# Cross attention 0: value products of two key tiles together; maxima kept in a table; keys copied ahead of the accumulator; other slots in the cosformer

## The chip, the cores and the metric

The kernel runs on one core of a Trainium2 chip. Its time is the device time of one execution in microseconds (us). A core has five engines with an instruction stream each, all in order: TensorE (PE in the profile, its weight loads PEld), VectorE (DVE), ScalarE (ACT), GpSimd (POOL) and SyncE (SP, which starts DMAs). They wait for one another by semaphores alone. SBUF holds operands; matmuls write to PSUM, which has eight banks of 128 partitions x 512 float32.

## The reference

A four-layer decoder on x of 1024 tokens x 128; each layer has a self attention, a cross attention over 6404 context rows, and a feed-forward part. The change touches two of the twelve parts. The first is the cross attention of layer 0 ("cross 0"), with 16 heads of 64:

```python
qw = (q_in @ Wq + bq).reshape(B, M, HEADS, QSIZE)
kw = (k_in @ Wk + bk).reshape(B, N, HEADS, QSIZE)
vw = (v_in @ Wv + bv).reshape(B, N, HEADS, KSIZE)
a = jnp.einsum('bmhd,bnhd->bhmn', qw, kw) / jnp.sqrt(jnp.float32(QSIZE))
a = jnp.where(key_mask[:, None, None, :], a, -jnp.inf)
a = jax.nn.softmax(a, axis=-1)
o = jnp.einsum('bhmn,bnhd->bmhd', a, vw).reshape(B, M, HEADS * KSIZE)
return o @ Wo + bo
```

The second is the self attention of layer 1, a "cosformer": queries and keys go through a relu and are weighted by the cosine and sine of their position, and a causal linear attention follows (16 heads of 64):

```python
num = jnp.einsum('bhi,bhij->bhj', qc, S_cos) + jnp.einsum('bhi,bhij->bhj', qs, S_sin)
den = jnp.sum(qc * z_cos + qs * z_sin, axis=-1)
den = jnp.maximum(den, 1e-06)[..., None]
return ((S_cos, S_sin, z_cos, z_sin), num / den)
```

## The kernel before, in words

**Cross 0** works on P = 8 pairs of heads, one after another; the two heads of a pair sit in partitions 0 to 63 and 64 to 127. The 6404 keys are C = 13 chunks of 512 (the last has 260), which are KT = 51 key tiles of 128: four to a chunk, three in the last. So there are N = 104 chunks in all and 408 tiles, counted by t over all pairs. Since 51 is odd, the tile that begins a chunk has an even t in pairs 0, 2, 4, 6 (called even pairs below) and an odd t in pairs 1, 3, 5, 7 (odd pairs).

Softmax needs each query's maximum before the exponentials. So two passes run at once, one chunk of each in a "turn" (`turns`, line 2188 on): the maxima pass works on chunk g, and the scores pass on chunk j = g - 14 (LAG is 14). Turns with g from 0 to 13 have maxima alone, g from 14 to 103 have both (90 turns), g from 104 to 117 have scores alone. A turn has as many steps s as chunk j has tiles. On PE (from line 2302) a step is, in order:

- `maxima(g, q)` (L2223): scores of query tile q of 128 against the chunk's 512 keys, in bf16, for both heads, to a pair of PSUM banks. There are eight q to a turn, so two to a step of four. While scores run too, they all use banks 4 and 5 (`maxima_bank`). DVE reduces both banks to one maximum for each head (L2405), and only then may PE write there again: `take_banks(4, ...)` waits for whoever used these banks last.
- `scores(j, s, half)` for both halves of the queries (L2236 in float32, L2238 which subtracts the maxima by a product with ones), to banks 0 and 1, and 2 and 3. ACT takes the exponential of each half into `Pr` (L2342), which has four slots by t.
- In step 0, one maxima call stands between the halves, and then `keys_and_values` (L2262, L2267) makes the next chunk's keys into bank 4 and values into bank 5; ACT copies the keys twice (L2362 float32, L2365 bf16) and the values once (L2371).
- Once for each pair, in a step of its own: `queries` (the projection), `rows` (maxima turned into rows), `sums` (row sums), `output`. All of these use banks 4 and 5 too.
- `products(t - 1)` (L2255): the values times the exponentials of the tile before, added up in banks 6 and 7.

The step's second maxima call stands behind the scores, right ahead of the products. POOL adds every exponential tile to the row sums (L2462, L2471). DVE merges the turn's maxima into `mx` (L2434 for the first chunk of a pair, L2437 later); at a pair's end it also negates them, rounds them to bf16 and keeps the rest (L2441, L2445, L2447), for `rows`. At a pair's end ACT copies the accumulator (L2356), once the pair's last products are done, ahead of the key copies of that step.

**The cosformer** (line 670 on) again has P = 8 pairs of heads, each with 12 units (PER): a unit u is up to 512 queries against a key tile of 128. PE makes the scores of unit n (L796), then one of the side jobs, then the products of unit n - 2 (L810). The side jobs all use banks 4 and 5 and stand at fixed u: queries and keys of the next pair (L767, L778), values in pair 0 (L785), column sums (L819), spreading of the inverted sums (L826) and the output projection (L833). DVE weights the scores (L948) and serves the side jobs between: values (L910), bound and inverse of the sums (L916 on, L921), scaling (L926), adding to X (L933, L935).

## Time and profile before

| | |
|---|---|
| three runs | 6390.63, 6393.21, 6397.06 us |
| profiled execution | 6391.79 us, its span 6390.0 us |
| mean granted TensorE clock | 0.915 |
| PE busy in the span | 5378.6 us, 84% |
| DVE, ACT, POOL busy | 3074.3, 3079.3, 2202.5 us |

The page of the profile gives this. A timeline shows the instructions of one engine in order of time, equal ones merged: start, duration, engine, line, what it writes and reads, the count, and in brackets how long the engine sat idle before it and who ended that wait. The duration of a merged matmul row runs to its modelled end, so it overlaps the next row's start; distances between starts are what counts. Cross 0's scores run from about 510 us to 2745 us of the span, the cosformer's loop from 2911 us to 3175 us.

### The profile page before, as it was taken

Reading aid. Unit: us, or ns where it says so; the run is one execution under the profiler, and the core shown is the slowest. Engines: PE = TensorE matmul, PEld = TensorE weight load, DVE = VectorE, ACT = ScalarE, POOL = GpSimd, SP = SyncE. Lnnn points to the kernel's source line nnn. Section 1 sums busy time; section 2 is a strip of 40 time slices with the busy share of each in tenths; the row PEclk is TensorE's granted clock in tenths of the full one; section 3 lists DMA queues with packets and bytes.
Section 4 is the critical chain, followed back from the end, with each engine's and each line's share of the span. In section 5 each row is a group of like instructions: output and inputs, shape, how many; then the busy total and the mean of one; then the engine's idle time right before and its main releaser. Section 6 shows DMA issues by size and latency. Waiting matters only on the chain. (4 is left out here: it accounts for less than half of the span.)

```text
span 6390.0 us, 69096 instructions
## 1 busy us (share of the span) xinstructions
PE 5378.6 (84%) x27758; PEld 1715.5 (27%) x27772; DVE 3074.3 (48%) x3482; ACT 3079.3 (48%) x3081; POOL 2202.5 (34%) x1100
## 2 busy tenths in 40 slices
PE   6658999999898999988888579998983588888879
PEld 2213333333333333332243211111431111111124
DVE  6575554555555554014541500000156999998613
ACT  3214444444454445521022379998121177777842
POOL 1006887878787878934533000000000000000000
PEclk7859999999999999989999789999796599999979
DMA  1000000000000000000000210000003000000001
GB/s 41 14 0 1 1 1 1 1 1 1 1 1 1 1 1 1 1 18 20 2 0 5 73 50 14 13 10 8 17 23 115 19 10 10 10 10 11 1 19 33
DMA packets 64814, 89.16 MB, mean 14 GB/s; under 512 B 9791, under 2 KB 49780, under 8 KB 62894
## 3 DMA queue, kind: packets, MB, share of 16 engines
q1 hardware_dynamic: 64494, 84.73, 4.2%
q8 instruction: 220, 3.60, 0.2%
q14 instruction: 100, 0.82, 0.0%
HBM read 59.33 MB, written 25.38 MB: 13 GB/s over the span
## 5 line engine op out<-in xcount | busy, mean ns | idle before, releaser
L2405 DVE TENSOR_REDUCE red<-ps 128x2 f32<-128x1024 f32 (+1 forms) x832 | 976.6, 1181 | 968.4 <-PE ps L2223 966.4
L2342 ACT ACTIVATE Pr<-ps,key_bias 128x1024 f32<-128x1024 f32 x816 | 897.6, 1115 | 1113.9 <-PE ps L2238 1111.4
L2462 POOL TENSOR_TENSOR Ps<-Ps,Pr 128x1024 f32<-128x1024 f32 x400 | 945.7, 2364 | 321.5 <-ACT Pr L2342 321.5
L2898 DVE TENSOR_REDUCE red<-ps 128x2 f32<-128x1024 f32 (+2 forms) x1102 | 961.3, 926 | 81.3 <-PE ps L2813 67.9
L2471 POOL TENSOR_TENSOR Ps<-Ps,Pr 128x1024 f32<-128x1024 f32 x400 | 949.9, 2375 | 32.8 <-ACT Pr L2342 32.7
L2876 ACT ACTIVATE Pr<-ps 128x1024 f32<-128x1024 f32 x816 | 786.2, 1021 | 226.4 <-PE ps L2823 225.3
L2236 PE MATMUL ps<-Q,Kr 64*128 64x512 f32 x3264 | 852.8, 601 | 0.0
L492 POOL MEMSET sel<- 16x2048 f32 (+1 forms) x2 | 2.7, 1368 | 2434.2 <-POOLq L89 2434.2
L2255 PE MATMUL ps<-Pr,Vc 128*64 128x512 f32 x3264 | 789.8, 605 | 0.0
L3001 ACT ACTIVATE Pr<-ps 128x2048 f32<-128x2048 f32 x467 | 726.2, 2025 | 1.6 <-PE ps L2967 1.6
L2813 PE MATMUL ps<-Kp,Q 52*128 52x512 bf16 (+1 forms) x1664 | 450.5, 411 | 225.0 <-DVE red L2898 149.1
L2223 PE MATMUL ps<-Kb,Qb 64*128 64x512 bf16 (+1 forms) x1664 | 332.6, 402 | 151.3 <-DVE red L2405 117.1
L2836 PE MATMUL ps<-Pr,V 128*9 128x512 f32 x3264 | 436.4, 606 | 0.0
L2980 PE MATMUL ps<-Pr,V 128*8 128x512 f32 x3264 | 427.2, 595 | 0.5 <-ACT Pr L3001 0.5
L2823 PE MATMUL ps<-Q,Kp 52*128 52x512 bf16 x1632 | 363.8, 386 | 12.2 <-ACT Pr L2876 11.8
L2236 PEld LDWEIGHTS ps<-Q,Kr 64*128 64x128 f32 x3264 | 312.2, 191 | 161.6 <-issue 122.7
L3010 DVE COPY Oc<-ps 128x512 f32<-128x512 f32 x8 | 5.5, 692 | 725.0 <-PE ps L2980 725.0
L2967 PE MATMUL ps<-Q,Kp 48*128 48x512 bf16 x1632 | 283.6, 385 | 82.6 <-ACT Pr L3001 55.2
L2813 PEld LDWEIGHTS ps<-Kp,Q 52*128 52x128 bf16 x1664 | 107.2, 94 | 799.9 <-DVE red L2898 712.8
L2238 PE MATMUL ps<-Qa,ones 64*128 64x512 bf16 x1632 | 313.7, 380 | 0.0
L2255 PEld LDWEIGHTS ps<-Pr,Vc 128*64 128x64 f32 x3264 | 198.0, 136 | 382.0 <-issue 290.5
L2223 PEld LDWEIGHTS ps<-Kb,Qb 64*128 64x128 bf16 x1664 | 80.4, 95 | 664.9 <-DVE red L2405 420.8
(563 smaller groups left out, 5245.8 us busy)
## 6 DMA issues: line engine op xcount, KB each, us to landing
L_dram_K<-parts SPq DMA_DIRECT2D x26, 384.0 KB, 2.9
Kp<-L_dram_K SPq DMA_DIRECT2D x16, 624.0 KB
L_dram_K<-parts SPq DMA_DIRECT2D x26, 256.0 KB, 2.4
Kp<-L_dram_K SPq DMA_DIRECT2D x16, 416.0 KB
w<-L_ffn_experts_w_dram SPq DMA_DIRECT2D x24, 256.0 KB, 3.0
ctx<-ctx_dram SPq DMA_DIRECT2D x13, 256.0 KB, 5.3
L_dram_K<-parts SPq DMA_DIRECT2D x26, 128.0 KB, 1.7
keep<-L_dram_mask SPq DMA_DIRECT2D x13, 256.0 KB, 3.5
```

The costliest lines, as they stand in the source:

```text
L2236: nc.tensor.matmul(ps[:, 2 * half + a, :], lhsT=Kr[head(a), j % 16, s * 128:(s + 1) * 128], rhs=Q[head(a), p % 3, sl], start=True, stop=False)
L2255: mm = nc.tensor.matmul(ps[head(a), 6 + half, :], lhsT=Vc[:, j % 3, at:at + 64], rhs=Pr[:, t % 4, half, a, :], start=False, stop=True, ski ...
L2342: nc.scalar.activation(Pr[:, t % 4, half].rearrange("p a n -> p (a n)"), ps[:, 2 * half:2 * half + 2, :].rearrange("p a n -> p (a n)"), AC ...
L2405: nc.vector.tensor_reduce(red[:, g % 2, q, :], ps[:, maxima_bank(g, q):maxima_bank(g, q) + 2, 0:ctx.keys_in(g % C)], AX, ALU.max).then_inc ...
L2462: nc.gpsimd.tensor_tensor(into, into, src, ALU.add).then_inc(*summed0.up())
L2471: nc.gpsimd.tensor_tensor(into, into, src, ALU.add).then_inc(*summed1.up())
L2813: mm = nc.tensor.matmul(ps[:, b + item - first, 0:keys], lhsT=Q[head(a), p, q * 128:(q + 1) * 128], rhs=Kp[head(a), p % 3, at:at + keys], ...
L2836: mm = nc.tensor.matmul(ps[at:at + 9, 6, :], lhsT=A.V[:, kt, 2 * p + a, :], rhs=Pr[:, t % 4, half, a, :], start=False, stop=True, skip_gro ...
L2876: nc.scalar.activation(Pr[:, t % 4, half].rearrange("p a n -> p (a n)"), ps[:, 2 * half:2 * half + 2, :].rearrange("p a n -> p (a n)"), AC ...
L2898: nc.vector.tensor_reduce(red_flat[:, g % 2, first:first + n], ps[:, b:b + n, 0:ctx.keys_in(g % C)], AX, ALU.max).then_inc(*reduced.up())
L2980: mm = nc.tensor.matmul(ps[at:at + 8, 7, :], lhsT=A.V[:, kt, 2 * p + a, :], rhs=Pr[:, i % 21, :], start=False, stop=True, skip_group_check ...
L3001: nc.scalar.activation(Pr[:, slot:slot + n, :].rearrange("p a n -> p (a n)"), ps[:, bank:bank + n, :].rearrange("p a n -> p (a n)"), ACT.S ...
```

## The change

On PE in cross 0 the products no longer stand in every step. In a step with odd t those of tiles t - 2 and t - 1 stand together; a step with even t has none. In DVE's part each turn's maxima go to their own column of a table `red` (two pairs deep, C columns), and `mx` is gone; at a pair's end two reductions over the table write the negated maxima, as float32 and as bf16, and a subtraction gives the rest. In ACT's part the accumulator's copy stands behind the key and value copies of its step. In the cosformer the side jobs stand at other u: the output of pair p - 2 at u = 1 of pair p (it was that of p - 1 at u = 11), queries at 3, keys at 5, values at 6 to 9 of pair 0, column sums at 6, the spreading at 11; the query relu of ACT stands behind the accumulator's copy.

```diff
@@ -843,22 +843,23 @@
         for n in range(N):
             p, u = n // PER, n % PER
             scores(n)
-            if p + 1 < P and u == 0:
+            if p >= 2 and u == 1:
+                output(p - 2)
+            if p + 1 < P and u == 3:
                 queries(p + 1)
-            if p + 1 < P and u == 2:
+            if p + 1 < P and u == 5:
                 keys(p + 1)
-            if p == 0 and u in (4, 6, 8, 10):
-                values(4 + (u - 4) // 2, 4)
-            if p and u == 4:
+            if p == 0 and u in (6, 7, 8, 9):
+                values(u - 2, 4)
+            if p and u == 6:
                 add_up(p - 1)
-            if p and u == 9:
+            if p and u == 11:
                 spread_out(p - 1)
-            if p and u == 11:
-                output(p - 1)
             if n >= 2:
                 products(n - 2)
         products(N - 2)
         products(N - 1)
+        output(P - 2)
         add_up(P - 1)
         spread_out(P - 1)
         output(P - 1)
@@ -880,11 +881,10 @@
         relate(0, 0, Q, bq, 4, q_set)
         relate(0, 1, K, bk, 6, k_set)
         for p in range(P):
-            if p + 1 < P:
-                relate(p + 1, 0, Q, bq, 4, q_set)
             if p:
                 copy_out(p - 1, 1)
             if p + 1 < P:
+                relate(p + 1, 0, Q, bq, 4, q_set)
                 relate(p + 1, 1, K, bk, 4, k_set)
             copy_out(p, 0)
         copy_out(P - 1, 1)
@@ -946,15 +946,15 @@
                 nc.vector.wait_ge(*weighed.at(n - 5))
                 nc.vector.wait_ge(*summed.at(n - 5))
             nc.vector.tensor_tensor(Pr[:, n % 6, :, 0:width], ps[:, b:b + 2, 0:width], table[:, x0:x0 + width].unsqueeze(1).to_broadcast([128, 2, width]), ALU.mult).then_inc(*weighted.up())
-            if p == 0 and u in (5, 7, 9, 11):
-                values(4 + (u - 5) // 2, 4)
-            if p and u == 4:
+            if p == 0 and 7 <= u < 11:
+                values(u - 3, 4)
+            if p and u == 6:
                 bound(p - 1)
-            if p and 5 <= u < 9:
-                invert(p - 1, u - 5)
-            if p and u == 10:
+            if p and 7 <= u < 11:
+                invert(p - 1, u - 7)
+            if p and u == 11:
                 scale(p - 1)
-            if p >= 2 and u == 0:
+            if p >= 2 and u == 1:
                 add_output(p - 2)
         add_output(P - 2)
         bound(P - 1)
...
@@ -2177,7 +2177,7 @@
     Pr = k.tile(stack, "Pr", [128, 4, 2, 2, HALF])
     Ps0, Ps1 = k.tile(stack, "Ps0", [128, 2, 2, HALF]), k.tile(stack, "Ps1", [128, 2, 2, HALF])
     Ur, over = k.tile(stack, "Ur", [128, S]), k.tile(stack, "over", [128, S])
-    mx, red, neg = k.tile(stack, "mx", [128, 8, 2]), k.tile(stack, "red", [128, 2, 8, 2]), k.tile(stack, "neg", [128, 8, 2])
+    red, neg = k.tile(stack, "red", [128, 2, 8, 2, C]), k.tile(stack, "neg", [128, 8, 2])
     mz = k.tile(stack, "mz", [128, 8, 2, 64], BF16)
     ones_f, zero_row = k.tile(stack, "ones_f", [128, 64]), k.tile(stack, "zero_row", [1, HALF], BF16)
     out_bias = k.tile(stack, "out_bias", [128, 1])
@@ -2325,8 +2325,12 @@
                     keys_and_values(g + 1, j + 1)
                 for item, p in others:
                     item(p)
-                if 0 <= j and 0 < t <= KT * P and (j < N or s == 0):
-                    products(t - 1)
+                if 0 <= j < N and t % 2:
+                    for u in range(max(0, t - 2), t):
+                        products(u)
+                if j == N and s == 0:
+                    for u in range(KT * P - 1 - KT * P % 2, KT * P):
+                        products(u)
 
     def act():
         def exponential(j, s, half):
@@ -2348,12 +2352,6 @@
                 if 0 <= j < N:
                     exponential(j, s, 0)
                     exponential(j, s, 1)
-                p = pair_for(g, s, LAG + C, 0)
-                if p is not None:
-                    nc.scalar.wait_ge(*weighed.at(KT * (p + 1)))
-                    if p:
-                        nc.scalar.wait_ge(*out_mm.at(p))
-                    nc.scalar.copy(Ur[:], ps[:, 6:8, :].rearrange("p a n -> p (a n)")).then_inc(*acc_copied.up())
                 if s == 0 and g + 1 < N:
                     i = g + 1
                     nc.scalar.wait_ge(*key_mm.at(i + 1))
@@ -2369,6 +2367,12 @@
                     if j + 1 >= 3:
                         nc.scalar.wait_ge(*weighed.at(KT * ((j - 2) // C) + min(KT, TPC * ((j - 2) % C + 1))))
                     nc.scalar.copy(Vc[:, (j + 1) % 3, 0:n], ps[:, 5, 0:n]).then_inc(*value_set.up())
+                p = pair_for(g, s, LAG + C, 0)
+                if p is not None:
+                    nc.scalar.wait_ge(*weighed.at(KT * (p + 1)))
+                    if p:
+                        nc.scalar.wait_ge(*out_mm.at(p))
+                    nc.scalar.copy(Ur[:], ps[:, 6:8, :].rearrange("p a n -> p (a n)")).then_inc(*acc_copied.up())
                 p = pair_for(g, s, C, 1)
                 if p is not None:
                     nc.scalar.wait_ge(*rows_mm.at(p + 1))
@@ -2400,9 +2404,9 @@
             for s in range(steps):
                 for q in maxima_at(g, s, steps):
                     nc.vector.wait_ge(*maxima_mm.at(8 * g + q + 1))
-                    if g >= 2 and q == 0:
-                        nc.vector.wait_ge(*merged.at(g - 1))
-                    nc.vector.tensor_reduce(red[:, g % 2, q, :], ps[:, maxima_bank(g, q):maxima_bank(g, q) + 2, 0:ctx.keys_in(g % C)], AX, ALU.max).then_inc(*reduced.up())
+                    if g >= 2 * C and g % C == 0 and q == 0:
+                        nc.vector.wait_ge(*rows_step.at(3 * (g // C) - 4))
+                    nc.vector.tensor_reduce(red[:, g // C % 2, q, :, g % C], ps[:, maxima_bank(g, q):maxima_bank(g, q) + 2, 0:ctx.keys_in(g % C)], AX, ALU.max).then_inc(*reduced.up())
                 p = pair_for(g, s, -1, 1)
                 if p is not None:
                     nc.vector.wait_ge(*query_mm.at(p + 1))
@@ -2428,23 +2432,16 @@
                     else:
                         nc.vector.wait_ge(*constant_set.at(1))
                         nc.vector.scalar_tensor_tensor(X[:], both.rearrange("p a n -> p (a n)"), out_bias[:, 0:1], X[:], ALU.add, ALU.add).then_inc(*x_added.up())
-            if 0 <= g < N:
+            if 0 <= g < N and g % C == C - 1:
+                p = g // C
                 nc.vector.wait_ge(*reduced.at(8 * (g + 1)))
-                if g % C == 0:
-                    nc.vector.tensor_copy(mx[:], red[:, g % 2]).then_inc(*merged.up())
-                else:
-                    nc.vector.wait_ge(*merged.at(g))
-                    nc.vector.tensor_tensor(mx[:], mx[:], red[:, g % 2], ALU.max).then_inc(*merged.up())
-                if g % C == C - 1:
-                    p = g // C
-                    nc.vector.wait_ge(*merged.at(g + 1))
-                    nc.vector.tensor_scalar(neg[:], mx[:], -1.0, None, ALU.mult).then_inc(*rows_step.up())
-                    nc.vector.wait_ge(*rows_step.at(3 * p + 1))
-                    if p:
-                        nc.vector.wait_ge(*rows_mm.at(p))
-                    nc.vector.tensor_copy(mz[:, :, :, 0], neg[:]).then_inc(*rows_step.up())
-                    nc.vector.wait_ge(*rows_step.at(3 * p + 2))
-                    nc.vector.tensor_tensor(mz[:, :, :, 1], neg[:], mz[:, :, :, 0], ALU.subtract).then_inc(*rows_step.up())
+                if p:
+                    nc.vector.wait_ge(*rows_step.at(3 * p))
+                    nc.vector.wait_ge(*rows_mm.at(p))
+                nc.vector.tensor_reduce(neg[:], red[:, p % 2], AX, ALU.max, negate=True).then_inc(*rows_step.up())
+                nc.vector.tensor_reduce(mz[:, :, :, 0], red[:, p % 2], AX, ALU.max, negate=True).then_inc(*rows_step.up())
+                nc.vector.wait_ge(*rows_step.at(3 * p + 2))
+                nc.vector.tensor_tensor(mz[:, :, :, 1], neg[:], mz[:, :, :, 0], ALU.subtract).then_inc(*rows_step.up())
 
     def pool():
         for g, j, steps in turns():
```

(The list of semaphore names in cross 0 loses `merged`.)

The order of PE in cross 0 from a step s = 0 on, in an even pair. Before (L2262 and L2267 are the next chunk's keys and values, L2255 the products, L2223 the maxima, L2236 and L2238 the scores):

```order
L2262 MATMUL ps<-ctx_masked,Wk 128x512
L2267 MATMUL ps<-Wv,ctx 128x128 x4
L2255 MATMUL ps<-Pr,Vc 64x512 x4
L2223 MATMUL ps<-Kb,Qb 128x512 x2
L2236 MATMUL ps<-Q,Kr 128x512 x2
L2238 MATMUL ps<-Qa,ones 128x512 x2
L2236 MATMUL ps<-Q,Kr 128x512 x2
L2238 MATMUL ps<-Qa,ones 128x512 x2
L2223 MATMUL ps<-Kb,Qb 128x512 x2
```

After, the same place on PE:

```order
L2262 MATMUL ps<-ctx_masked,Wk 128x512
L2267 MATMUL ps<-Wv,ctx 128x128 x4
L2223 MATMUL ps<-Kb,Qb 128x512 x2
L2236 MATMUL ps<-Q,Kr 128x512 x2
L2238 MATMUL ps<-Qa,ones 128x512 x2
L2236 MATMUL ps<-Q,Kr 128x512 x2
L2238 MATMUL ps<-Qa,ones 128x512 x2
L2223 MATMUL ps<-Kb,Qb 128x512 x2
```

The products behind keys and values are gone from here: the next step's maxima follow the value matmuls. The rows of PE that follow, to the end of step 2, before:

```order
L2255 MATMUL ps<-Pr,Vc 64x512 x4
L2223 MATMUL ps<-Kb,Qb 128x512 x2
L2236 MATMUL ps<-Q,Kr 128x512 x2
L2238 MATMUL ps<-Qa,ones 128x512 x2
L2236 MATMUL ps<-Q,Kr 128x512 x2
L2238 MATMUL ps<-Qa,ones 128x512 x2
L2223 MATMUL ps<-Kb,Qb 128x512 x2
L2255 MATMUL ps<-Pr,Vc 64x512 x4
L2223 MATMUL ps<-Kb,Qb 128x512 x2
L2236 MATMUL ps<-Q,Kr 128x512 x2
L2238 MATMUL ps<-Qa,ones 128x512 x2
```

After, from the products behind step 1 on:

```order
L2255 MATMUL ps<-Pr,Vc 64x512 x8
L2223 MATMUL ps<-Kb,Qb 128x512 x2
L2236 MATMUL ps<-Q,Kr 128x512 x2
L2238 MATMUL ps<-Qa,ones 128x512 x2
L2236 MATMUL ps<-Q,Kr 128x512 x2
L2238 MATMUL ps<-Qa,ones 128x512 x2
L2223 MATMUL ps<-Kb,Qb 128x512 x4
L2236 MATMUL ps<-Q,Kr 128x512 x2
L2238 MATMUL ps<-Qa,ones 128x512 x2
L2236 MATMUL ps<-Q,Kr 128x512 x2
L2238 MATMUL ps<-Qa,ones 128x512 x2
```

Eight product matmuls stand where four did. The products of the step behind them (even t) are gone, and its last maxima call (two matmuls) stands next to the first of the following step, four in a row.

The order of ACT where a pair's accumulator is copied. Before (L2356 is that copy, L2362, L2365 and L2371 are the key and value copies, L2342 the exponentials):

```order
L2342 ACTIVATE Pr<-ps,key_bias 128x1024 x4
L2356 COPY Ur<-ps 128x1024
L2362 ACTIVATE Kr<-ps,bk 128x512
L2365 ACTIVATE Kb<-ps,bk 128x512
L2371 COPY Vc<-ps 128x512
L2342 ACTIVATE Pr<-ps,key_bias 128x1024 x2
L2383 COPY over<-ps 128x1024
```

After (L2375 is the accumulator's copy, L2360, L2363 and L2369 are those of keys and values, L2346 the exponentials):

```order
L2346 ACTIVATE Pr<-ps,key_bias 128x1024 x4
L2360 ACTIVATE Kr<-ps,bk 128x512
L2363 ACTIVATE Kb<-ps,bk 128x512
L2369 COPY Vc<-ps 128x512
L2375 COPY Ur<-ps 128x1024
L2346 ACTIVATE Pr<-ps,key_bias 128x1024 x2
L2387 COPY over<-ps 128x1024
```

The accumulator's copy moved behind the three copies that bank 4 and 5 wait for.

In the cosformer's PE order one scores call and one products call stood between the output projection (L833) and the queries (L767); now two of each do. Between queries and keys (L778) it is two of each both times. The value calls of pair 0 (L785) had two scores and two products calls between them, and now have one of each.

## Rows read from the trace of the kernel before

**Rows 1.** Windows: length; busy us of PE, PEld, DVE, ACT, POOL; clock; DMA
```profile
490.00:2496.00 2006.00, 1865.90 (x9576) 681.85 (x9576) 1044.97 (x905) 948.71 (x992) 1617.31 (x708) 0.98 0.00 1
2496.00:2745.00 249.00, 248.41 (x1232) 89.08 (x1232) 24.04 (x20) 128.71 (x126) 243.29 (x107) 1.00 0.00 1
2911.00:3175.00 264.00, 240.09 (x976) 74.89 (x976) 139.46 (x154) 25.00 (x30) 152.76 (x96) 0.97 0.00 1
```

**Rows 2.** Timeline of PE in one plain turn: start, duration, line, [idle <-releaser]
```profile
1219.93 0.39 PE L2223 MATMUL ps<-Kb,Qb 64*128 64x512 bf16 x2
...
1221.78 0.39 PE L2223 MATMUL ps<-Kb,Qb 64*128 64x512 bf16 x2 [0.38 <-DVE red L2405]
...
1223.49 1.12 PE L2262 MATMUL ps<-ctx_masked,Wk 128*128 128x512 f32 x2 [0.25 <-DVE red L2405]
1224.45 1.05 PE L2267 MATMUL ps<-Wv,ctx 128*128 128x128 f32 x8
1225.43 1.94 PE L2255 MATMUL ps<-Pr,Vc 128*64 128x512 f32 x8
1227.31 0.39 PE L2223 MATMUL ps<-Kb,Qb 64*128 64x512 bf16 x2
1227.53 1.02 PE L2236 MATMUL ps<-Q,Kr 64*128 64x512 f32 x4
...
1229.68 0.38 PE L2223 MATMUL ps<-Kb,Qb 64*128 64x512 bf16 x2
1229.99 1.94 PE L2255 MATMUL ps<-Pr,Vc 128*64 128x512 f32 x8
1231.86 0.39 PE L2223 MATMUL ps<-Kb,Qb 64*128 64x512 bf16 x2
...
1240.96 0.39 PE L2223 MATMUL ps<-Kb,Qb 64*128 64x512 bf16 x2
```

**Rows 3.** Timeline of DVE and of ACT in the same turn
```profile
1219.43 1.15 DVE L2437 TENSOR_TENSOR mx<-mx,red 128x16 f32<-128x16 f32 x1
...
1227.74 1.23 DVE L2405 TENSOR_REDUCE red<-ps 128x2 f32<-128x1024 f32 x1 [4.30 <-PE ps L2223]
...
1225.81 0.59 ACT L2371 COPY Vc<-ps 128x512 f32<-128x512 f32 x1
```

**Rows 4.** Timeline of PE: the first tile, and the end of one head pair
```profile
517.17 0.39 PE L2223 MATMUL ps<-Kb,Qb 64*128 64x512 bf16 x2 [1.03 <-ACT Vc L2371]
...
1346.29 0.39 PE L2223 MATMUL ps<-Kb,Qb 64*128 64x512 bf16 x2
...
1353.25 0.61 PE L2223 MATMUL ps<-Kb,Qb 64*128 64x512 bf16 x2 [5.49 <-DVE red L2405]
...
1371.10 0.38 PE L2223 MATMUL ps<-Kb,Qb 64*128 64x512 bf16 x2
...
1372.80 0.39 PE L2223 MATMUL ps<-Kb,Qb 64*128 64x512 bf16 x2 [1.32 <-DVE red L2405]
...
1385.72 0.39 PE L2223 MATMUL ps<-Kb,Qb 64*128 64x512 bf16 x2 [2.85 <-ACT Vc L2371]
...
1403.48 0.39 PE L2223 MATMUL ps<-Kb,Qb 64*128 64x512 bf16 x2
```

**Rows 5.** Timeline of DVE at the same end
```profile
1345.27 1.94 DVE L2437 TENSOR_TENSOR mx<-mx,red 128x16 f32<-128x16 f32 x1
...
1349.54 2.29 DVE L2445 CAST mz<-neg 128x16 bf16<-128x16 f32 x1
1351.87 0.23 DVE L2447 TENSOR_TENSOR mz<-neg,mz 128x16 bf16<-128x16 f32 x1
```

**Rows 6.** Timeline of PE in the cosformer
```profile
2926.73 1.98 PE L785 MATMUL ps<-Wv,h 128*128 128x512 f32 x4 [1.03 <-DVE V L910]
...
2971.12 1.96 PE L833 MATMUL ps<-Ur,wo 128*128 128x512 f32 x4 [0.58 <-DVE Ur L926]
...
2977.45 3.47 PE L767 MATMUL ps<-h,Wq 128*128 128x512 f32 x4 [2.52 <-DVE X L935]
```

More of the change, by code:

```diff
@@ L2163, in cross_0 @@
     (weights, zeroed, constant_mm, constant_set, reduced, key_mm, value_mm, query_mm, maxima_mm, rows_mm, sums_mm, out_mm, key_set, key_copied, value_set,
-     query_set, query_copied, merged, rows_step, rows_set, sums_set, scored, exp_done, weighed, acc_copied, summed0, summed1, inverse_step, x_added) = k(
+     query_set, query_copied, rows_step, rows_set, sums_set, scored, exp_done, weighed, acc_copied, summed0, summed1, inverse_step, x_added) = k(
         "weights", "zeroed", "constant_mm", "constant_set", "reduced", "key_mm", "value_mm", "query_mm", "maxima_mm", "rows_mm", "sums_mm", "out_mm", "key_set",
-        "key_copied", "value_set", "query_set", "query_copied", "merged", "rows_step", "rows_set", "sums_set", "scored", "exp_done", "weighed", "acc_copied",
+        "key_copied", "value_set", "query_set", "query_copied", "rows_step", "rows_set", "sums_set", "scored", "exp_done", "weighed", "acc_copied",
         "summed0", "summed1", "inverse_step", "x_added")
```

## The prediction

> **What bounds the kernel now.** I read the windows first, for the stages that the change touches. While cross 0 runs both passes PE is busy 1865.90 of 2006.00 us at a granted clock of 0.98; POOL has 1617.31 us of work, DVE 1044.97, ACT 948.71 [rows 1]. So PE's own order sets the time, and each wait of PE is paid. In the last 14 turns PE is busy 248.41 of 249.00 us, but POOL 243.29 [rows 1]: what PE gives back there POOL nearly takes. In the cosformer PE is busy 240.09 of 264.00 us [rows 1]. The chain of waits covers only the program's end and says nothing on these stages, so I went to PE's timeline of one plain turn, by the distances between starts. The reader is to see this: a maxima call issues in 0.22 us (1227.31 to 1227.53); both halves of the scores take 1229.68 - 1227.53 = 2.15, or 1.08 each; from the last maxima over the products to the next step's maxima it is 2.18 (1229.68 to 1231.86); a plain step takes 4.55, and the whole turn 1219.93 to 1240.96, 21.03 us [rows 2].
>
> **Products together (gain).** Eight product matmuls at full clock take four times 512 columns for each of two halves, concurrently for two heads; by the trace from 1229.99 to 1231.86, 1.87 us, of which I count 1.72 as work (twice a score half without its ones product: 1.08 - 0.22 = 0.86) and 0.15 as the way out; the way in costs 0.31 - 0.22 = 0.09 [rows 2]. A group that joins another saves 0.24 us, one behind keys and values 0.15. The Trainium skill, "TensorEngine Tiling (Array Packing)", section Tiling Modes (Key Properties), says that a change of tiling mode drains TensorE; the rows agree, with 0.24 us for two changes, and by it this edit alone would be a gain of some 40 us.
>
> **What the products hid (loss).** A maxima call may issue when its predecessor's banks are reduced. DVE starts 0.43 us after the call (1227.31 to 1227.74) and takes 1.23 [rows 2, 3]; where two calls stand together in the trace, the second starts 1.70 us after the first, with PE idle 1.32 beyond the modelled end [rows 4]. Before, products of 2.18 us stood between a step's last call and the next step's first: no wait. In a step with even t and s > 0 they are gone, and two calls adjoin: 1.71 - 0.22 = 1.49 us each. In a step 0 with even t, the next call follows the value matmuls and waits for ACT's three copies: they end at 1226.40, 2.91 us after the key matmul's start, while PE is ready at 1225.37 or so; 1.04 us [rows 2, 3]. The very first tile, which has no products before it, shows that wait: idle 1.03 us for the value copy [rows 4]. Nothing else stands behind a waiting maxima call that could hide it: PE is in order, so both score halves and the next exponentials are late too.
>
> **A plain turn.** The merge of 1.15 us goes from DVE, which held the first reduction back: 1.85 between the first two maxima becomes 1.71, -0.14 [rows 2, 3]. Even pair: -0.14, -0.15 and -0.24 for two joined groups, +1.04 +1.49 = +2.0 us. Odd pair: -0.14, -0.48, +2.98 = +2.36. Of the 90 turns with both passes, I take 11 plain ones in pair 0 and 9 each in pairs 2, 4, 6 (38, +76), 27 in pairs 1, 3, 5 (+64). The turn with the query projection and the one with the output go alike in even pairs (+1.7 each, 7 of them, +12); in odd pairs the DVE work behind output and inverse adds to the exposed wait (+2.3 and +4.0, 3 of each, +19). Sum: +171.
>
> **The pair's end.** Today DVE's merge, negation and cast each last about 2 us for 16 elements (1.94 and 2.29 shown, while POOL works) against 0.23 for the last one, and hold PE 5.49 us; after it the maxima takes 0.61 instead of 0.39, the lower clock [rows 4, 5]. From 1346.29 to 1403.48 the last turn of a pair and the first of the next take 57.2 us [rows 4]. The change leaves two reductions and one subtraction. A reduction over 13 x 16 elements is not in the trace; between 0.23 [rows 5] and 1.23 [rows 3], I take 0.4, since 208 elements are a fifth of 1024. The subtraction may still last 2.3, so 0.5 to 2.8 us stay in odd pairs, while in even ones eight products (3.4 us) cover it. The key copies ahead of the accumulator's take away the wait of 2.85 us and what lower clock follows it [rows 4]. But between an odd and an even pair the last product stands in step 1 together with the first of the next pair, which overwrites the accumulator: ACT's copy of about 1 us then stands between the two, some 1.5 us idle, and the exponentials queued behind it are late. I walk both turns with the distances above (1.71 from call to call where a reduction decides, 2.38 where scores do, 1.94 for keys and values, 3.6 for eight products; starts in us). Even to odd: maxima 0, 1.71, keys 3.42, maxima 6.40, 8.11, 9.82, rows 11.53, products 12.0, maxima 15.6, 17.98, 19.69, next turn 21.40; in that: maxima 0, 1.71, keys 3.42, products 5.36, maxima 8.95, 10.66, sums 12.37, maxima 15.7 (ACT's copy of the sums), 18.1, products 18.4, maxima 22.3, 24.7, end 26.4 and 0.5 for an inverse: 48.3 us, -8.9. Odd to even: maxima 0, 3.4 (the subtraction), keys 5.1, products 7.05, maxima 10.64, 12.35, 14.06, rows 15.77, maxima 17.5, 19.9, 21.6, products 21.9, next turn 25.5; in that: maxima 0, 1.71, keys 3.42, maxima 6.40, 8.11, sums 9.82, last product 11.7, first of the pair behind the copy 14.9, maxima 18.1, 20.5, 22.2, 24.6, products 24.8, end 28.4: 53.9 us, -3.3. Three of each: -37 us. The Trainium skill, "SBUF — State Buffer", section Who interferes with whom, has a copy, cast or tensor_scalar and a tensor_tensor of two SBUF inputs wait for GpSimd, and says tensor_reduce never does; the long rows agree. If the new reductions waited all the same, each would cost up to 2.3 us more, some 25 us over the ends.
>
> Turns with maxima alone lose small merges, and the tail half its groups (27 x 0.24 = 6.5 us of PE), which POOL's 243.29 of 249 [rows 1] lets through only in part: -3 for both. Cross 0: +171 - 37 - 3 = +131 us.
>
> **The cosformer.** Before, queries waited 2.52 us for the X addition and then took 3.47 instead of 1.98 us, the lower clock [rows 6]; that goes in 5 pairs: -20. The output's wait of 0.58 [rows 6] goes in 7: -4. The inverse's wait is about the same. Against it: the values of pair 0 stood two units apart and waited 1.03 us [rows 6]; now one unit apart they wait for weighting and value addition on DVE, about 2.7 us three times, +6 net and perhaps the lower clock, +7. At the end the output now stands ahead of the column sums: +2, and +2 at the spreading. Sum -13, bounds -24 and +5.
>
> **Sum.** 6391.79 + 131 - 13 = 6510; the profiled execution is 1.4 us under the median of 6393.21, so 6511 us.
>
> **The rivals.**
> - Clock. The new waits drop PE to 1.2 GHz again and again. For it: after 5.49, 2.85 and 2.52 us idle the matmuls that follow are slow [rows 4, 6]. Against it: after 1.32, 1.03 [rows 4] and 1.03 [rows 6] the next are of full speed (0.39; 1.98), and no new wait in a plain turn is over 1.5 us. If one slow stretch of 3 us came with each turn, that is +1.5 us to +3 in 90 turns, 6650 to 6780. The Trainium skill, "TensorE: Matmul & The Clock Gate", section Part 1: The HAM clock gate, has idle PE lead to the lower clock; the rows show it only from 2.5 us on.
> - The change wins. The wait decides: if DVE's release reached PE so that two adjoining calls cost nothing (less than 0.24 us each, the price of a switch), only the gains would be left: switches -38, merges -10, pair ends -50, tail -3, cosformer -13, so 6279 us. Against it stands the distance of 1.70 us in the rows, in the same code with the same banks [rows 4].
> - Half is hidden: waits overlap others (first maxima of a turn, POOL's slots), the loss falls to +40 to +70 and the time to 6430 to 6460. For it speaks that each turn has 0.8 us of waits in step 0 already; against it, that in the walk they stay beside the new ones.
> - Nothing moves (gains equal losses), 6393: this needs 1.49 to be 0.8.
>
> **How the numbers follow.** Forecast (6470 to 6570) 0.72; clock 0.12; half hidden 0.08; wins 0.05; the rest between. No change means within 0.2%, 13 us, about what a measurement can tell. Faster 0.05, same 0.02, slower 0.93. The range 6445 to 6610 takes in an occasional slow stretch and the bounds of the pair ends.
>
> **What would show it.** Plain turns of about 23.0 us in even and 23.4 in odd pairs; idle time of about 1.3 us, put down to the reduction, ahead of the second of two adjoining maxima calls, some 120 times; about 1 us put down to the value copy; eight products in 3.6 us; the reductions at a pair's end well under 1 us; no wait at the cosformer's queries. Wrong would be a turn under 21 us, or matmuls of the lower clock inside plain turns.

## The result and the profile after

The changed kernel takes 6505.41 us (median of 4 runs, 6502.82 to 6507.91); the kernel before 6391.92 us (median of 4, 6383.82 to 6397.06). The ratio is 1.0179, with a 95% interval of 1.0161 to 1.0196: slower by 113 us, against a forecast of 6511 us. The profiled execution of each kernel (6504.59 and 6391.79 us) lies within 2 us of its median, so the traces can be compared as they are.

The page after: the span, the maxima reduction and the maxima matmuls (line, engine, out<-in, count, busy and mean ns, idle before them and who ended it):

```profile
span 6502.9 us, 68800 instructions
...
L2409 DVE TENSOR_REDUCE red<-ps 128x2 f32<-128x1024 f32 (+1 forms) x832 | 977.3, 1184 | 1208.6 <-PE ps L2223 1208.6
...
L2223 PE MATMUL ps<-Kb,Qb 64*128 64x512 bf16 (+1 forms) x1664 | 331.7, 400 | 308.9 <-DVE red L2409 224.3
```

Idle time of PE itself ahead of its maxima matmuls rose to 308.9 us. The same group on the page of before:

```profile
L2223 PE MATMUL ps<-Kb,Qb 64*128 64x512 bf16 (+1 forms) x1664 | 332.6, 402 | 151.3 <-DVE red L2405 117.1
```

The difference of 157.6 us is more than the whole loss. PE's waits in the stage of both passes, by who ended them (us in total, times, longest), before (512 to 2509 us of the span) and after (511 to 2637):

```profile
PE ps L2223 <- DVE red L2405: 82.8, 106, 5.5
PE ps L2223 <- ACT Vc L2371: 18.1, 7, 2.8
...
PE ps L2223 <- DVE red L2409: 190.9, 225, 1.8
PE ps L2223 <- ACT Vc L2369: 52.6, 51, 1.1
```

Of the waits for the reduction, 113 are of 1.3 us after and 12 before: 101 new ones, where the prediction looked for some 120 in all. Waits for the value copy of 1.0 to 1.1 us went from 1 to 50.

The windows after, for the three stages of [rows 1] (length; busy us of PE, PEld, DVE, ACT, POOL; clock; DMA share and rate):

```profile
490.00:2630.00 2140.00, 1836.93 (x9600) 698.53 (x9602) 939.28 (x816) 950.29 (x995) 1626.65 (x710) 0.99 0.00 1
2637.00:2886.00 249.00, 244.53 (x1216) 91.06 (x1216) 12.74 (x14) 128.54 (x126) 242.43 (x107) 1.00 0.00 1
3040.00:3297.00 257.00, 239.44 (x985) 74.79 (x984) 144.57 (x157) 24.20 (x30) 152.73 (x96) 0.98 0.00 1
```

PE has less to do (1836.93 us in place of 1865.90) and a clock as high as before (0.99, before 0.98), but the window is over 130 us longer. By the first exponential and the last maxima matmul the stage runs from 511.7 to 2636.8 us of the span, before from 512.4 to 2508.8: +128.7 us. From there to the last copy of the accumulator it is 254.2 us against 250.9, +3.2. The cosformer, from its first scores to its last output projection, takes 256.4 us against 273.7, -17.3. With -0.7 us ahead of the first exponential these make 113.9 us; the spans differ by 112.9, so the rest of the program gives -1.0.

### The profile page after: what moved, and what is told of

Same layout as the page of the kernel before. It is cut to its first block and busy times, and to the rows that moved or that the text cites. A ratio compares the mean times of both kernels' runs of the same rounds, so it can differ in the third digit from the quotient of the medians.

```text
span 6502.9 us, 68800 instructions
## 1 busy us (share of the span) xinstructions
PE 5334.6 (82%) x27758; PEld 1728.4 (27%) x27772; DVE 2960.4 (46%) x3378; ACT 3077.4 (47%) x3081; POOL 2205.0 (34%) x1100
## 5 line engine op out<-in xcount | busy, mean ns | idle before, releaser
L2346 ACT ACTIVATE Pr<-ps,key_bias 128x1024 f32<-128x1024 f32 x816 | 897.0, 1114 | 1236.2 <-PE ps L2238 1235.2
L2236 PE MATMUL ps<-Q,Kr 64*128 64x512 f32 x3264 | 844.9, 594 | 4.5 <-ACT Pr L2346 2.9
L2255 PE MATMUL ps<-Pr,Vc 128*64 128x512 f32 x3264 | 745.7, 598 | 0.0
L2223 PE MATMUL ps<-Kb,Qb 64*128 64x512 bf16 (+1 forms) x1664 | 331.7, 400 | 308.9 <-DVE red L2409 224.3
L2236 PEld LDWEIGHTS ps<-Q,Kr 64*128 64x128 f32 x3264 | 308.4, 189 | 159.9 <-issue 122.7
L2255 PEld LDWEIGHTS ps<-Pr,Vc 128*64 128x64 f32 x3264 | 216.1, 136 | 422.4 <-issue 343.8
L2238 PE MATMUL ps<-Qa,ones 64*128 64x512 bf16 x1632 | 313.0, 377 | 0.0
L2223 PEld LDWEIGHTS ps<-Kb,Qb 64*128 64x128 bf16 x1664 | 82.1, 94 | 749.0 <-DVE red L2409 402.4
```

What stands on the lines that cost most here:

```text
L2236: nc.tensor.matmul(ps[:, 2 * half + a, :], lhsT=Kr[head(a), j % 16, s * 128:(s + 1) * 128], rhs=Q[head(a), p % 3, sl], start=True, stop=False)
L2255: mm = nc.tensor.matmul(ps[head(a), 6 + half, :], lhsT=Vc[:, j % 3, at:at + 64], rhs=Pr[:, t % 4, half, a, :], start=False, stop=True, ski ...
L2346: nc.scalar.activation(Pr[:, t % 4, half].rearrange("p a n -> p (a n)"), ps[:, 2 * half:2 * half + 2, :].rearrange("p a n -> p (a n)"), AC ...
```

## Where it went: the rows that answer

A plain turn of an even pair on PE, from key matmul to key matmul (start, duration, engine and line, idle before):

```profile
1269.69 1.13 PE L2262 MATMUL ps<-ctx_masked,Wk 128*128 128x512 f32 x2 [0.25 <-DVE red L2409]
1270.65 1.05 PE L2267 MATMUL ps<-Wv,ctx 128*128 128x128 f32 x8
1272.74 0.39 PE L2223 MATMUL ps<-Kb,Qb 64*128 64x512 bf16 x2 [1.03 <-ACT Vc L2369]
...
1275.10 0.40 PE L2223 MATMUL ps<-Kb,Qb 64*128 64x512 bf16 x2
1275.42 3.65 PE L2255 MATMUL ps<-Pr,Vc 128*64 128x512 f32 x16
1279.01 0.39 PE L2223 MATMUL ps<-Kb,Qb 64*128 64x512 bf16 x2
...
1281.38 0.38 PE L2223 MATMUL ps<-Kb,Qb 64*128 64x512 bf16 x2
1283.09 0.39 PE L2223 MATMUL ps<-Kb,Qb 64*128 64x512 bf16 x2 [1.32 <-DVE red L2409]
...
1285.77 3.65 PE L2255 MATMUL ps<-Pr,Vc 128*64 128x512 f32 x16
1289.36 0.39 PE L2223 MATMUL ps<-Kb,Qb 64*128 64x512 bf16 x2
...
1292.79 1.13 PE L2262 MATMUL ps<-ctx_masked,Wk 128*128 128x512 f32 x2 [0.25 <-DVE red L2409]
```

Step 0 has no products. Its successor's maxima call waits 1.03 us for the value copy, at 1272.74. Behind step 1 come eight products in one piece, 3.59 us from start to start (1275.42 to 1279.01); two groups of [rows 2] take 1.87 each, so 3.74. Step 2 has no products either: the calls of 1281.38 and 1283.09 adjoin, 1.71 us apart, with PE idle 1.32 us, just as the two adjoining calls of [rows 4]. The turn is 1292.79 - 1269.69 = 23.10 us; it was 21.03 [rows 2]. The key matmul that follows still waits for a reduction (0.25 at 1292.79), so the new waits come on top of step 0's old ones and don't replace them. In odd pairs, where two pairs of calls adjoin, the turn is 23.39 us by the distances between ACT's key copies. The plain turns of even and of odd pairs keep these two lengths, 23.10 and 23.39 us, over the whole cross, but for one of 23.61 in each odd pair.

DVE at a pair's end, which answers to [rows 5], and what POOL did meanwhile:

```profile
1401.82 0.37 DVE L2441 TENSOR_REDUCE neg<-red 128x16 f32<-128x208 f32 x1
1402.11 0.36 DVE L2442 TENSOR_REDUCE mz<-red 128x16 bf16<-128x208 f32 x1
1402.51 2.31 DVE L2444 TENSOR_TENSOR mz<-neg,mz 128x16 bf16<-128x16 f32 x1
...
1402.37 2.36 POOL L2459 TENSOR_TENSOR Ps<-Ps,Pr 128x1024 f32<-128x1024 f32 x1
```

The two reductions over the 13 columns take 0.37 and 0.36 us while POOL works; the merge and the cast took 1.94 and 2.29 [rows 5]. The subtraction, which reads two tensors of SBUF, still lasts 2.31 us and ends at 1404.82, when the POOL addition that began at 1402.37 is over (1404.73). The rule of the Trainium skill ("SBUF — State Buffer", section Who interferes with whom) that on this chip a tensor_reduce doesn't wait for GpSimd is borne out by these rows.

PE at the end of an odd pair: the first two maxima calls of the last turn, the first zeroing product of the next pair, the first call of the turn after:

```profile
1095.22 0.39 PE L2223 MATMUL ps<-Kb,Qb 64*128 64x512 bf16 x2 [0.80 <-DVE red L2409]
...
1098.06 0.39 PE L2223 MATMUL ps<-Kb,Qb 64*128 64x512 bf16 x2 [1.37 <-DVE red L2409]
...
1134.85 0.60 PE L2248 MATMUL ps<-zero_row 1*128 1x512 bf16 x2 [1.11 <-ACT Ur L2375]
...
1148.12 0.39 PE L2223 MATMUL ps<-Kb,Qb 64*128 64x512 bf16 x2
```

ACT in the same stretch:

```profile
1125.92 0.59 ACT L2369 COPY Vc<-ps 128x512 f32<-128x512 f32 x1
1133.78 1.01 ACT L2375 COPY Ur<-ps 128x1024 f32<-128x1024 f32 x1 [7.27 <-PE ps L2255]
```

The wait of 5.49 us [rows 4] is down to 1.37, and the clock stays up: 0.39 us for the call where it was 0.61. At the end of pair 3, in the step after `rows`, it did fall once, after waits of 1.32 and 1.11 us:

```profile
1729.20 0.64 PE L2281 MATMUL ps<-ident,mz 128*64 128x128 bf16 x16 [1.32 <-DVE red L2409]
1730.95 0.39 PE L2223 MATMUL ps<-Kb,Qb 64*128 64x512 bf16 x2 [1.11 <-ACT Qa L2381]
1731.17 1.69 PE L2236 MATMUL ps<-Q,Kr 64*128 64x512 f32 x4
```

Such scores take 1.02 us elsewhere, the clock from 1732 to 1734 us was granted at 0.50, and this pair's end is 1.70 us longer than those of pairs 1 and 5. It is the only such stretch in the stage once the scores run steadily; the kernel before has twelve, two at each pair's end.

From 1095.22 to 1148.12 the two turns take 52.90 us. What remains is the coupling that the order makes: ACT's accumulator copy waits 7.27 us for the pair's last products, with the next exponentials behind it, and PE's zeroing product waits 1.11 us for that copy. The end of an even pair, by the first call of its last turn and that of the turn after the next:

```profile
1404.56 0.39 PE L2223 MATMUL ps<-Kb,Qb 64*128 64x512 bf16 x2
...
1452.30 0.39 PE L2223 MATMUL ps<-Kb,Qb 64*128 64x512 bf16 x2 [1.33 <-DVE red L2409]
```

That is 47.74 us, against 57.2 before [rows 4]. The end of an odd pair took 56.2 us before, by the same two calls.

The cosformer on PE, which answers to [rows 6]: the values of pair 0, an output projection and the next queries:

```profile
3061.11 1.98 PE L785 MATMUL ps<-Wv,h 128*128 128x512 f32 x4 [2.46 <-DVE V L910]
...
3067.62 1.98 PE L785 MATMUL ps<-Wv,h 128*128 128x512 f32 x4 [2.46 <-DVE V L910]
...
3073.64 1.98 PE L785 MATMUL ps<-Wv,h 128*128 128x512 f32 x4 [2.19 <-DVE V L910]
...
3138.91 1.98 PE L833 MATMUL ps<-Ur,wo 128*128 128x512 f32 x4
...
3143.57 1.98 PE L767 MATMUL ps<-h,Wq 128*128 128x512 f32 x4
```

No wait stands ahead of these L833 and L767 calls any more, and the queries take 1.98 us. The values of pair 0 wait 2.46, 2.46 and 2.19 us where they waited 1.03, 0.39 and 0.55. The spreading of the inverted sums waits 0.42 us, as before.

## The experiments

In each, "the kernel before" stands for runs of it on the same chip.

**e1, products together.** The products together can't stand alone: at the end of an odd pair the last products would stand behind a maxima call that waits for the key copies, these would stand behind the accumulator's copy, and that copy waits for these products, which is a circle. So the earlier key copies are in it too.

```diff
-                if 0 <= j and 0 < t <= KT * P and (j < N or s == 0):
-                    products(t - 1)
+                if 0 <= j < N and t % 2:
+                    for u in range(max(0, t - 2), t):
+                        products(u)
...
(the last product behind the last scores, and ACT's accumulator copy behind the key and value copies)
```

> Kernel before plus products together and the accumulator's copy behind the key copies (the first can't stand without the second: an odd pair's end would wait in a circle). No maxima table, cosformer as before. My theory (what the products hid: 1.49 us between adjoining maxima calls, 1.04 us behind keys and values): the changed kernel's 6505 without the cosformer's -17 and without the table's gain of some 55 us, so about 6575 us. Plain turns of 23.2 to 23.6 us. Rival, that the time was added by the new maxima table or by the cosformer's slots: 6390 or less.

Measured: 6573.17 us (6564.81 to 6583.44), ratio 1.0269 (1.0245 to 1.0293). The plain turns are 23.09 and 23.86 us; I expected at most 23.6, since in odd pairs the old merge delays the first call's reduction, which now stands right behind another: some 30 waits of 0.7 us stand ahead of maxima calls here, where the changed kernel has one. One row of PE at an odd pair's end shows what the table later takes away:

```profile
1114.02 0.61 PE L2223 MATMUL ps<-Kb,Qb 64*128 64x512 bf16 x2 [6.19 <-DVE red L2409]
```

This kernel's part is the whole of the loss and more. The rival that the table or the cosformer cost the time is out.

**e2, the maxima table alone.**

```diff
-    mx, red, neg = k.tile(stack, "mx", [128, 8, 2]), k.tile(stack, "red", [128, 2, 8, 2]), k.tile(stack, "neg", [128, 8, 2])
+    red, neg = k.tile(stack, "red", [128, 2, 8, 2, C]), k.tile(stack, "neg", [128, 8, 2])
...
+                nc.vector.tensor_reduce(neg[:], red[:, p % 2], AX, ALU.max, negate=True).then_inc(*rows_step.up())
+                nc.vector.tensor_reduce(mz[:, :, :, 0], red[:, p % 2], AX, ALU.max, negate=True).then_inc(*rows_step.up())
```

> Kernel before plus the maxima table alone. My theory: each turn loses 0.14 us (merge gone, 77 plain turns, -11), each of 6 pair ends 7 to 8.7 us (wait of 5.49 us and the lower clock behind it), small merges -2: about 6332 us. Rival, that the two reductions over the table wait for GpSimd as the merge did: pair ends gain 2 us only, about 6370 us.

Measured: 6335.04 us (6332.02 to 6352.03), ratio 0.9906 (0.9882 to 0.9930). A plain turn is 20.91 us, the turn around a pair's end 22.4 in place of 28.6 to 29.1. The gain of 58 us is the one forecast for reductions that don't wait (61); had they waited, it would have been 23.

**e3, key copies ahead of the accumulator's copy, alone.**

```diff
-                p = pair_for(g, s, LAG + C, 0)
-                if p is not None:
-                    nc.scalar.wait_ge(*weighed.at(KT * (p + 1)))
...
                     nc.scalar.copy(Vc[:, (j + 1) % 3, 0:n], ps[:, 5, 0:n]).then_inc(*value_set.up())
+                p = pair_for(g, s, LAG + C, 0)
+                if p is not None:
+                    nc.scalar.wait_ge(*weighed.at(KT * (p + 1)))
```

> Kernel before plus the accumulator's copy behind the key and value copies. My theory: the wait of 2.85 us and some 1.6 us of lower clock go at 6 pair ends, -27: about 6365 us. Rival, that the accumulator's later copy holds the next pair's first products: no gain, 6392 us.

Measured: 6367.49 us (6364.35 to 6372.67), ratio 0.9946 (0.9926 to 0.9966): 25 us less, against 27 expected and none by the rival.

**e4, the cosformer's slots alone** (the first three pieces of the change's diff).

```diff
+            if p >= 2 and u == 1:
+                output(p - 2)
-            if p + 1 < P and u == 0:
+            if p + 1 < P and u == 3:
                 queries(p + 1)
```

> Kernel before plus the cosformer's other slots alone. By the changed kernel's trace the loop is 17 us shorter: about 6375 us. Forecast in the prediction was -13. Rival, that its gain is lost outside the loop: 6392 us.

Measured: 6374.60 us (6366.73 to 6379.55), ratio 0.9963 (0.9947 to 0.9980). The loop is 256.4 us long here too.

**e5, the change without products together.**

```diff
-                if 0 <= j < N and t % 2:
-                    for u in range(max(0, t - 2), t):
-                        products(u)
...
+                if 0 <= j and 0 < t <= KT * P and (j < N or s == 0):
+                    products(t - 1)
```

> The changed kernel with products in every step again: table, keys first and cosformer's slots stay. If the three gains stand beside each other (-60, -27, -17) about 6288 us, faster than both kernels. Rival, that each hides behind the same wait at a pair's end, so that they don't add: 6320 or more.

Measured: 6294.93 us (6291.24 to 6311.65), ratio 0.9859 (0.9838 to 0.9880). Against the kernel before, the three edits gain 58, 25 and 18 us by themselves, 102 in sum, and 96 together (92 on another chip, below), so they nearly add. Seen from the changed kernel, undoing the one edit gives back 210 us: that is its price, nearly twice the loss that the whole change shows.

**e6, the maxima call between the score halves.** If the price is the distance between two calls on the same banks, moving a call must lower it with no work taken away. Behind a step 0 the score half that goes ahead also fills the wait for the value copy.

```diff
+                late = 0 <= j < N and s > 0 and t % 2 == 1 and not others
-                for q in items[:1]:
+                for q in items[:0 if late else 1]:
                     maxima(g, q)
...
-                for q in items[1:between]:
+                for q in items[0 if late else 1:between]:
                     maxima(g, q)
```

> The changed kernel; in a step with odd t and s > 0 without a call of its own the first maxima call stands between the two score halves instead of ahead of them. It then has 1.08 us of scores behind its predecessor, and waits 0.41 instead of 1.49, but so does the next one: -0.67 us in each such step, -1.3 us in an even pair's turn where the wait for key copies goes too: -81 us in all, about 6424 us. Rival, that the added time is not these waits but the longer products or exponentials that come late: 6505 us.

Measured: 6440.45 us (6428.45 to 6447.64), ratio to the kernel before 1.0073 (1.0054 to 1.0091), so 65 us under the changed kernel. The rival of this run, 6505 us, is out. PE in one such pair of steps:

```profile
1247.51 0.38 PE L2223 MATMUL ps<-Kb,Qb 64*128 64x512 bf16 x2
...
1249.22 0.39 PE L2223 MATMUL ps<-Kb,Qb 64*128 64x512 bf16 x2
...
1250.93 0.39 PE L2223 MATMUL ps<-Kb,Qb 64*128 64x512 bf16 x2 [0.25 <-DVE red L2410]
1251.25 3.65 PE L2255 MATMUL ps<-Pr,Vc 128*64 128x512 f32 x16
1254.84 0.39 PE L2223 MATMUL ps<-Kb,Qb 64*128 64x512 bf16 x2
```

The three calls stand 1.71 us apart, and the second has scores in front of it in place of idle time. The pair of steps that took 10.35 us in the changed kernel (1279.01 to 1289.36 above) takes 9.71 (1245.13 to 1254.84); cross 0, from the first exponential to the last accumulator copy, is 72.7 us shorter. The profiled execution began cross 0 some 15 us late, in parts that no kernel here changes, which is why its whole time, the longest of the four, shows less than the stage. Whether the other three began late is not on record. The forecast of 81 was a little high; a plain turn of an odd pair takes 22.74 us, one of an even pair 21.87.

**e7a and e7b, shorter reductions.** The same edit in the changed kernel and in the one before; it leaves out the maxima of half of each bank's keys. In the changed kernel (before, `red` has no column index):

```diff
-                    nc.vector.tensor_reduce(red[:, g // C % 2, q, :, g % C], ps[:, maxima_bank(g, q):maxima_bank(g, q) + 2, 0:ctx.keys_in(g % C)], AX, ALU.max).then_inc(*reduced.up())
+                    nc.vector.tensor_reduce(red[:, g // C % 2, q, :, g % C], ps[:, maxima_bank(g, q):maxima_bank(g, q) + 2, 0:256], AX, ALU.max).then_inc(*reduced.up())
```

> The changed kernel, with each maxima reduction over 256 of the 512 keys of a bank (the maxima of the others are left out), so about 0.70 instead of 1.23 us; PE's work is the same. My theory: each adjoining pair of calls waits 0.53 less (126 of them, -67) and step 0 waits 0.8 less in 77 turns (-63): about 6375 us. Beside the same edit in the kernel before, the loss falls from 113 to about 55 us. Rival, that the loss does not hang on the reduction: it stays 113.

> The kernel before with the same shorter reductions (maxima of half the keys left out). Only step 0's waits go, 0.95 us in 77 turns, -73, and some at pair ends: about 6315 us. Turns of 20.1 us.

Measured: 6312.95 us (6305.74 to 6314.87) and 6251.18 us (6246.18 to 6255.88). Two adjoining calls of e7a on PE:

```profile
1245.00 0.38 PE L2223 MATMUL ps<-Kb,Qb 64*128 64x512 bf16 x2
1246.17 0.39 PE L2223 MATMUL ps<-Kb,Qb 64*128 64x512 bf16 x2 [0.79 <-DVE red L2409]
```

They are 1.17 us apart in place of 1.71, with PE idle for 0.79 us in place of 1.32. The loss between the two is 62 us, down from 113; I expected 55. Both kernels are faster by some 62 us than I wrote, since I left out the 14 turns that have maxima alone, in which DVE is busy 118.13 of 150 us before (350 to 500 us of the span): the first exponential starts at 459.6 us of the span in both, 52 us earlier than in the changed kernel (511.7). The other 10 us are not traced to a cause. So the loss hangs on the reduction's length: 51 of its 113 us go with half of it. What stays is the rest of each wait between adjoining calls (0.79 us idle) and the value copy's wait (1.03 us), less the switches saved and the three gains.

**e8, the second call of step 0 on other banks** (from e5). This one looks for the next gain: step 0 waits 0.41 us twice for banks 4 and 5, while banks 0 and 1 are free between a tile's first exponential and the next tile's scores.

```diff
-        return (4, 0, 2)[(8 * i + q) % 3] if i < LAG else 4
+        return (4, 0, 2)[(8 * i + q) % 3] if i < LAG else 0 if q == 1 else 4
...
+                after_keys = s == 0 and g >= LAG
...
                 if s == 0:
                     keys_and_values(g + 1, j + 1)
+                for q in items[1:] if after_keys else ():
+                    maxima(g, q)
```

> The changed kernel with products in every step again, and in step 0 of each turn with scores the second maxima call no longer stands between the score halves on banks 4 and 5 but behind the value matmuls on banks 0 and 1, which the first exponential has left by then. If the waits on banks 4 and 5 in step 0 (0.41 us ahead of the second call and 0.41 ahead of the key matmul) are all that such a call costs, a plain turn falls from 20.91 to 20.1 us: -0.8 us in some 83 turns, about 6229 us. Rival, that the exponential or the next step's scores then wait for this bank: 6295 us or more.

> The kernel of table, keys first and cosformer's slots, without products together, once more beside the other on the same chip: 6295 us as before.

Measured on one chip: e8 6247.05 us (6243.67 to 6260.27), ratio 0.9764 (0.9747 to 0.9780); e5 again 6302.54 us (6301.05 to 6303.81), ratio 0.9853 (0.9836 to 0.9869). A plain turn of e8 on PE:

```profile
1131.61 1.13 PE L2262 MATMUL ps<-ctx_masked,Wk 128*128 128x512 f32 x2
1132.57 1.05 PE L2267 MATMUL ps<-Wv,ctx 128*128 128x128 f32 x8
1133.56 0.39 PE L2223 MATMUL ps<-Kb,Qb 64*128 64x512 bf16 x2
1133.88 1.94 PE L2255 MATMUL ps<-Pr,Vc 128*64 128x512 f32 x8
1135.74 0.39 PE L2223 MATMUL ps<-Kb,Qb 64*128 64x512 bf16 x2
...
1151.87 1.12 PE L2262 MATMUL ps<-ctx_masked,Wk 128*128 128x512 f32 x2
```

No wait is left in it, and it takes 1151.87 - 1131.61 = 20.26 us, 0.64 under e5's 20.91. I expected 20.1: the call now stands between the values and the products, and from its start to the products it is 0.32 us, 0.1 more than the 0.22 of a call among scores. The forecast of 6229 us was 18 too low: 8 of it because e5 itself came out at 6302.54 here in place of 6295, the rest because a turn gains 0.64 and not 0.8 (cross 0 is 53.8 us shorter than in e5 again). This is the fastest version: 148 us under the kernel before on the same chip, 258 under the changed one.

## Why the prediction was right

Point by point, by its own steps:

- **Plain turns.** Forecast +2.0 and +2.36 us, measured, with 21.04 as the usual turn before, +2.06 and +2.35. Over 38 and 27 turns that is +78 and +63, against +76 and +64. This term carried the prediction. It came from one distance of the old trace, the two adjoining calls of [rows 4], and from one wait that the old trace held in its very first tile [rows 4].
- **Products together.** A joined group saves 0.15 us by the rows above (3.59 against 3.74); with the way in of 0.09 [rows 2], which the second group no longer has, that is the 0.24 of the forecast. By this price the gain is some 40 us (worked out, no run has it alone); it is only smaller than what it lays bare.
- **Reductions at the pair's end.** 0.37 us each against the 0.4 taken; the subtraction's 2.31 is the 2.3 allowed. Pair ends take 47.7 and 52.9 us (54.6 at the end of pair 3, with the slow stretch), forecast 48.3 and 53.9. The prediction took 57.2 us for both kinds before, but the odd ends took 56.2; so the gains are 9.4 and 3.3, forecast 8.9 and 3.3, and -37 us in all came out by two errors of 1 us that cancel.
- **Both passes together.** Forecast +134 (171 less 37), measured +128.7. With the start and the tail, where the errors are the other way, cross 0 is at +131.2 against +131: that close a fit is luck.
- **The tail.** This step failed, by little: I counted half the product groups as a gain of 3 us together with the start (measured -0.7 there), but the tail is 3.2 us longer. POOL has 242.43 us of work in 249.00 there (243.29 before [rows 1]), so PE's saving can't show, and a step with eight products delivers its successor's exponentials later. The products together are the cause: the tail is 254.2 us in e1, e6 and e7a as well, and 250.3 to 250.9 in every kernel with products in each step. That it comes about through the late exponentials is argued from the timeline alone.
- **The cosformer.** Forecast -13, measured -17.3. The values' waits add up to 7.11 us where they were 1.97, +5.1 in place of the +7 taken; the end, taken at +4, came by difference to some +2. The lower clock that I allowed for pair 0's values didn't come in this trace, nor in those of e4 and e5. It came in four others with the same cosformer (e5 again, e6, e7a, e8), whose loop takes 258.0 to 259.7 us in place of 256.4. That the profiled execution was spared is luck, worth up to 3.3 us.

The rivals: the lower clock did not come in plain turns (granted 0.99 in the stage, one slow stretch at a pair's end); the change did not win, because the distance of 1.70 us holds wherever two calls adjoin; and the loss was not half hidden. That nothing moves would have needed more than the prediction says: by its own sum, with some 105 adjoining calls (92 of them in plain turns) for 118 us, the wait of 1.49 would have to be about 0.4, not 0.8.

Two readings behind the clock rival need mending. [rows 4] does not show slow matmuls after the wait of 2.85 us: the call right behind it is fast there (0.39), and the slow ones begin within the scores after it. The second score half, in the kernel before, takes 1.95 us in place of 1.02:

```profile
1387.97 1.95 PE L2236 MATMUL ps<-Q,Kr 64*128 64x512 f32 x4
```

And "only from 2.5 us on" holds for the rows that it shows, not for the chip: see the last section.

## What to carry to other kernels

Before work is gathered to save switches, ask what each scattered piece stands in front of: here some 2 us of products hid the 1.5 us that a call still has to wait for the reduction, or the last 1.0 us of three copies, and gathering it saved 0.24 us a time and cost up to 1.49. Where two equal calls happen to adjoin in the old trace, their distance is what each new such place will cost: here 1.70 us, in 12 places before and 113 after. And a change of several parts can lose while most of its parts win: run them apart, since three of these four gain 96 us together, and the fourth costs 210.

## What the runs showed of the hardware

- The length of a wait alone does not tell which of the two clock levels (1.2 and 2.4 GHz) comes after it. In the kernel before, the cosformer's queries waited 2.52 us once [rows 6] and 2.45 four times, and the matmuls behind each wait went at half speed. The value matmuls after the change waited 2.46, 2.46 and 2.19 us and took 1.98 us each in three traces (the changed kernel, e4, e5). In e6 and e8 the same third wait of 2.19 us was followed by the lower level (granted 0.50), in e5 again the second wait of 2.46 (the first row below is of e8, the second of e5 again). In the changed kernel the scores at 1731.17 slowed down after waits of 1.32 and 1.11 us. What decides is not shown here.

```profile
2828.70 3.55 PE L785 MATMUL ps<-Wv,h 128*128 128x512 f32 x4 [2.19 <-DVE V L910]
...
2859.25 3.68 PE L785 MATMUL ps<-Wv,h 128*128 128x512 f32 x4 [2.46 <-DVE V L910]
```

- A DVE reduction over 208 elements a partition in SBUF took 0.37 us beside a working POOL, and a subtraction of 16 elements 2.31; 0.23 us is what such a subtraction took once before [rows 5].
- A maxima call costs 0.22 us of PE among scores (1227.31 to 1227.53 [rows 2]), and 0.1 more between the value matmuls and the products (0.32, e8).
- From a maxima call over its reduction of 1.23 us to the next call on the same two banks it is 1.71 us; with a reduction of 0.69 us it is 1.17 (e7a).
